# A group's tail in the attention layer is spread over more block steps

## The chip, the cores and the metric

The kernel runs on one core of a Trainium2 chip. The metric is the device time of one launch in microseconds (us), as the median of several launches. Before the change it is 2312.75 us, the median of 3 launches between 2312.53 and 2313.29.

## The reference

Four residual layers on a graph of 4096 nodes with 256 features, each preceded by a normalisation of the rows and a ReLU. Only the second layer, the attention, is touched:

```
h = maximum(layernorm(x), 0)
x = x + L0(h, adj)                       # A_norm @ (A2 @ h @ W.T)
h = maximum(layernorm(x), 0)
x = x + L1(h, adj)                       # the attention, below
h = maximum(layernorm(x), 0)
x = x + L2(h, adj)
h = maximum(layernorm(x), 0)
x = x + L3(h, adj)

L1:  h = x @ weight
     h_norm = h / maximum(norm(h), 1e-8)
     attn_logits = h_norm @ h_norm.T + log(adj + 1e-8)
     out = softmax(attn_logits, axis=1) @ h + bias
```

The numerators of the softmax are `(adj + 1e-8) * exp(cosine)`. `adj` is 4096 x 4096 in f32.

## The kernel before, in words

**Tiling.** Rows are taken in 8 groups of 512 (`NG`), the inner dimension in 32 blocks of 128 (`NB`), a group's rows in four row blocks of 128 (`GB`). f32 operands are split into two f16 halves, "hi" and "lo", and each product is three f16 matmuls: hi by hi, hi by lo, lo by hi. The program goes through six passes; pass 2 (`ATT`) is the attention, written out without loops. In the trace it lies between about 723 and 1320 us.

**One block step of the attention.** In step j of group g four engines work hand in hand:

- TensorE makes the cosines of block j + 3 (`LEAD`) in a PSUM bank (`similarity`, L1389 to L1391, six matmuls of 512 columns). The cosine matrix is symmetric, so blocks that an earlier group has made are fetched back and only transposed (L1375, four small matmuls). Then it multiplies block j (`product`, L1084 to L1086, twelve matmuls), which needs the lo half of the numerators of block j.
- ScalarE takes the exponential of block j where it is computed (L1846), then makes the hi half of block j - 1 (L1867).
- VectorE makes the numerators of block j (`numerators`, L2487, or L2494 in pieces) and then the lo half of block j - 1 (`lo_of_numerators`, L2502). Each engine executes its instructions in the order in which they are written.
- Beside that a sum S4 for a later pass is made out of the same blocks of `adj`: VectorE makes it in steps with j mod 4 = 3 (L2001) and its lo half in steps with j mod 4 = 1 (L2007), ScalarE its hi half in steps with j mod 4 = 0 (L1526). Groups 0 and 1 have one VectorE instruction more at each of the two (L1982, L1992).

**A group's tail.** When a group is through, its result goes through a chain of small pieces, which is interleaved with the block steps of the next group by the tables `ATT_PLACES`, one on each engine, indexed by the step j. Of the tail of group g - 1, in group g:

- VectorE: `epi0`, `epi1` (`attended`, L2149: x plus result over denominator, two row blocks each), `stats0`, `stats1` (L2401, two row blocks each), `stats2` (L2405 to L2408), `h0`, `h1` (L2414, lo half of the normalised rows), `mix0`, `mix1`, `mix2`, `W2` (L2310 to L2332, the combinations of the small product's result that the next pass multiplies by).
- ScalarE: `ev` (L1591), `h0` to `h3` (L1788, L1790), `W0` and `W1` (copies of the small products out of PSUM, L1715, and with `W1` the hi half of three quarters of them, L1738), `W2` (L1744).
- TensorE: `"W0W1"` at step `W_AT`, the small products by the next layer's weights (24 matmuls, L1295 to L1297), into the bank `psW` and into `psT`, which otherwise is one of three banks for the cosines. In the seven steps from `W_AT` on only the two banks `psS` are used for cosines.
- SyncE's queue, in half steps H (two block steps each): `send_x` stores x, `turn_h` turns the normalised rows with a DMA transpose (L778). Both wait for VectorE, and loads that come later in the queue wait behind them.

Group 7 (the last) has its own third table: the tail of group 6, but in place of the mixes two pieces that prepare the next pass (`sum`, `split0`).

Of the kernel before, what the change touches and what calls it, by code (L numbers as in the profile page):

```python
# [41 lines left out]
F = 256  # L42
P = 128
NB = N // P
GB = 4
# [37 lines left out]
def build(nc, x, adj_t, w0, wg, bias_g, w2, bias_2, w3a, w3b, sent, sums, ready, x_mid, directs, out):  # L83
    f32, f16 = mybir.dt.float32, mybir.dt.float16
    ALU, ACT = mybir.AluOpType, mybir.ActivationFunctionType

    ctx = ExitStack()
    with ctx:
        def sb(name, shape, dt):
            return ctx.enter_context(nc.sbuf_tensor(name, shape, dt))  # L90
# [4 lines left out]
        def sem(name):  # L95
            return ctx.enter_context(nc.semaphore(name))
# [15 lines left out]
        xs = left[:, spare:spare + GB * F].rearrange("p (b n) -> p b n", b=GB)  # L112
# [33 lines left out]
        ev = sb("ev", [P, GB, F + 1], f32)  # L146
# [50 lines left out]
        rden = sb("rden", [P, GB], f32)  # L197
# [60 lines left out]
        scaled = sem("scaled")  # L258
# [77 lines left out]
        def at(passes, p, g, per=1, k=1):  # L336
            return (g + NG * passes.index(p)) * per + k
# [118 lines left out]

            return sum(NB - GB * h for h in range(g)) + j - GB * g + 1

        W_AT = 23
        SIM_SLOT, SIM_BEFORE = [], []  # L460
        for n in range(NG * NB):
            last = {s: m for m, s in enumerate(SIM_SLOT)}
            s = min((0, 1) if n < NB or W_AT <= n % NB < W_AT + 7 else (0, 1, 2), key=lambda s: last.get(s, s - 3))
            SIM_SLOT.append(s)
# [100 lines left out]
        def _(sp):  # L565
# [76 lines left out]
            def store_s3(g, c):  # L642

                sp.wait_ge(s3_split, g * NC + c + 1)
                sp.dma_start(ready[bass.ds(g * (NC * P) + c * P, P), 4 * QUAD:6 * QUAD], out3[c % 4])\
                    .then_inc(s3_stored[c % 4], 16)

            def load_s2(n):

                if n >= S2_LATER * NC + 3:  # L650
                    sp.wait_ge(s4_split, n - 2)
                else:
                    sp.wait_ge(sum_ready, at(SELF, 1, NG - 1))
                sp.dma_start(s4_of(n), sums[n * P:(n + 1) * P, :]).then_inc(s2_back[n % 4], 16)
# [11 lines left out]
            def send_x(p, g):  # L666

                if p == 1:
                    sp.wait_ge(bias_added, g + 1)
                else:  # L670
                    sp.wait_ge(x_ready, at(RES, p, g))
                rows = x_rows(p, g).rearrange("p b n -> p (b n)")
                sp.dma_start(x_mid[bass.ds(g * P, P), :], rows).then_inc(x_stored, 16)
# [99 lines left out]
            def turn_h(p, g):  # L773

                sp.wait_ge(h_ready, at(SMALL, p, g))
                sp.wait_ge(small_ready, at(SMALL, p, g - 1, 2, 2))
                sp.sem_inc(turning, 1)
                sp.dma_start_transpose(hT[:, :, :], hsp[:, :, :, :].rearrange("p b s n -> p (b s n)"))\  # L778
                    .then_inc(hT_landed, 16)

            def turn_gn(g):

                sp.wait_ge(gn_ready, at([1], 1, g, GB, GB))
                sp.sem_inc(turning, 1)
                sp.dma_start_transpose(gnT[:, bass.ds(g * GB * 2 * FB, GB * 2 * FB), :],
                                       hsp[:, :, :, :].rearrange("p b s n -> p (b s n)")).then_inc(gnT_landed, 16)
# [124 lines left out]
            def att_extra(g, H):  # L911

                n = g * NH + H
                if n == 9 + NH:
                    for k in range(3):
                        load_s2(S2_LATER * NC + k)
                if g == 0:
                    if H < 4:
                        store_s3(NG - 1, H + 4)
                    if H == 4:  # L920
                        turn_gn(NG - 2)
                        send_x(1, NG - 2)
                    elif H == 8:
                        turn_h(1, NG - 1)
                    elif H == 10:
                        send_x(1, NG - 1)
                    elif H == 12:
                        turn_gn(NG - 1)
                else:
                    if H == 8:  # L930
                        send_x(ATT, g - 1)
                    elif H == 12:
                        turn_h(ATT, g - 1)

                if H == NH - 1:
                    fetch_x(ATT, g)

                if H % 2 == 0 and n >= 6:
                    store_s4((n - 6) // 2)
                    if (n - 6) // 2 < S2_LATER * NC:  # L940
                        store_s2((n - 6) // 2)
                    else:
                        load_s2((n - 6) // 2 + 3)
# [132 lines left out]
        def _(pe):  # L1076
# [173 lines left out]
            def small(p, g, r):  # L1250
# [10 lines left out]
                else:  # L1261

                    pe.wait_ge(hT_landed, 16 * at(TURN, p, g))
                    if p == ATT:
                        sim_taken(pe, max(n for n in range((g + 1) * NB + W_AT) if SIM_SLOT[n] == 2 or n == 0))

# [43 lines left out]

            ATT_PLACES = [{14: "W0W1"}, {W_AT: "W0W1"}]

# [34 lines left out]
            def similarity(g, j):  # L1347
# [7 lines left out]
                if SIM_SLOT[n] == 2:  # L1355
                    if n < NB + W_AT:
                        pe.wait_ge(gn_ready, at([1], 1, NG - 1, GB, GB))
                    else:
                        pe.wait_ge(small_copied, at(COPIED, ATT, (n - W_AT) // NB - 1, GB, GB))
                if computed(g, j):  # L1360
# [93 lines left out]
        def _(act):  # L1454
# [303 lines left out]
            def stage(name, p, g):  # L1758
# [12 lines left out]
                elif p in COPIED and name == "W2":  # L1771
# [2 lines left out]

            PLACES = {0: ["ev"], 4: ["h"], 5: ["k"], 6: ["W0", "W1"], 7: ["n0", "n1", "W2"]}
            ATT_PLACES = [{2: ["ev"], 10: ["h"], 15: ["W0"], 16: ["W1"], 18: ["n0"], 19: ["n1"]},
                          {2: ["ev"], 13: ["h0"], 14: ["h1"], 15: ["h2"], 16: ["h3"], 25: ["W0"], 26: ["W1"], 30: ["W2"]},
                          {2: ["ev"], 13: ["h0"], 14: ["h1"], 15: ["h2"], 16: ["h3"], 25: ["W0"], 26: ["W1"], 30: ["split0"]}]

            def att_h(g, b):  # L1780

# [144 lines left out]
        def _(dve):  # L1926
# [214 lines left out]
            def attended(g, i):  # L2141

                if i == 0:
                    dve.wait_ge(ev_ready, at(ALL, ATT, g, GB, GB))
                    nc.vector.reciprocal(rden[:, :], ev[:, :, F]).then_inc(den_ready, 1)
                    dve.wait_ge(x_back, 16 * at(BACK, ATT, g))
                    dve.wait_ge(den_ready, g + 1)
                for b in (2 * i, 2 * i + 1):
                    nc.vector.scalar_tensor_tensor(xs[:, b, :], ev[:, b, 0:F], rden[:, b:b + 1], xs[:, b, :],  # L2149
                                                   ALU.mult, ALU.add).then_inc(scaled, 1)  # L2150

            def last_mix():

# [54 lines left out]
            def epilogue(p, g):  # L2208

                if p in STR:  # L2210
                    dve.wait_ge(mixed, at(STR, p, g, NP, NP))
                    if p in ADDED:

                        dve.wait_ge(d_back, 16 * at(ADDED, p, g))
                        nc.vector.tensor_tensor(oq, oq, d_in, ALU.add).then_inc(turned_sum if p == TURNED else preact, 1)
                        return
                else:
                    dve.wait_ge(ev_ready, at(ALL, p, g, GB, GB))
                if p in SELF:

                    dve.wait_ge(own_ready, at(SELF, p, g))
                    nc.vector.tensor_tensor(o[:, :, :], ev[:, :, 0:F], own[:, :, :], ALU.add).then_inc(sum_ready, 1)
                    nc.vector.tensor_scalar(rowm[:, :], ev[:, :, F], 0.0, None, ALU.is_gt).then_inc(row_ready, 1)
                    nc.vector.tensor_scalar(rowc[:, :], ev[:, :, F], TINY, None, ALU.max).then_inc(row_ready, 1)
                    dve.wait_ge(sum_ready, at(SELF, p, g))
                if p == 1:
                    for b in range(GB):
                        nc.vector.tensor_scalar(o[:, b, :], o[:, b, :], d[:, blocks(g, b)], None, ALU.mult)\
                            .then_inc(scaled, 1)
                elif p == 2:  # L2230
                    for i in range(2):
                        attended(g, i)
                elif p == 3:
                    for b in range(GB):
                        nc.vector.scalar_tensor_tensor(o[:, b, :], o[:, b, :], dinv[:, blocks(g, b)], b2[:, :],
                                                       ALU.mult, ALU.add).then_inc(scaled, 1)
# [110 lines left out]
            def stage(name, p, g):  # L2347
# [28 lines left out]
                elif p == 1 and name in ("n0", "n1"):  # L2376
# [3 lines left out]
                      7: ["n0", "n1", "W2"]}  # L2380
            ATT_PLACES = [{2: ["ev"], 4: ["epi"], 6: ["x"], 7: ["stats"], 10: ["h"], 12: ["bias"], 15: ["W0"], 16: ["W1"],
                           18: ["n0"], 19: ["n1"]},
                          {4: ["epi0"], 6: ["epi1"], 8: ["stats0"], 9: ["stats1"], 10: ["stats2"],
                           16: ["h0"], 18: ["h1"], 26: ["mix0"], 28: ["mix1"], 30: ["mix2"], 31: ["W2"]},
                          {4: ["epi0"], 6: ["epi1"], 8: ["stats0"], 9: ["stats1"], 10: ["stats2"],
                           16: ["h0"], 18: ["h1"], 29: ["sum"], 31: ["split0"]}]
            LATE = {0: ["mix0", "mix1"], 1: ["mix2"], 2: ["W2"]}

            def att_piece(name, g):
# [245 lines left out]
```

## Time and profile before

| what | value |
|---|---|
| median of 3 launches | 2312.75 us |
| profiled launch | 2313.05 us, span 2311.3 us |
| TensorE (PE) matmul busy | 2289.8 us, 99% |
| VectorE (DVE) busy | 1693.5 us, 73% |
| ScalarE (ACT) busy | 1127.9 us, 49% |
| TensorE idle in the attention, by its waits | 4.0 us |

An instruction's row has its start, its duration, engine, line, what it writes and reads. In brackets stand the idle time of the engine before it and who ended that. Matmuls overlap: those of 258 columns last 0.27 us each but start every 0.11 us. Neighbours on VectorE and ScalarE overlap by about 0.1 us too, so that what one costs there is the distance between starts.

### The profile page before, as it was taken

What the parts mean: (1) busy time and instruction counts of PE and PEld (TensorE: products, weight loads), DVE (VectorE), ACT (ScalarE), POOL (GpSimd) and SP (SyncE); (2) the same over time, 40 slices, a digit from 0 to 9 for tenths busy, and PEclk for the clock granted to TensorE, in tenths of its full rate; (3) what the DMA queues carried; (4) which work ended last, traced back from release to release, by engine and by line L of the source; (5) the groups of instructions that cost most, each with busy time, mean ns of one, the idle gap of its engine ahead of it and who ended that gap; (6) DMA issues with size and microseconds to landing.
All of it is one profiled execution on the core that took longest, in us unless ns stands there. A gap on an engine that the chain in (4) does not pass through costs nothing.

```text
span 2311.3 us, 61483 instructions
## 1 busy us (share of the span) xinstructions
PE 2289.8 (99%) x24200; PEld 1896.5 (82%) x24200; DVE 1693.5 (73%) x2709; ACT 1127.9 (49%) x1806; POOL 145.9 (6%) x139
## 2 busy tenths in 40 slices
PE   7999999999999999999999999999999999999999
PEld 4555557888888677778888899999988888899999
DVE  7678677676677788778888876776766667667666
ACT  7444434445544555555555555455454444433332
POOL 3300110111111000000000000000000000000000
PEclk9999999999999999999999999999999999999999
DMA  9989998889887898989999998998998998999998
GB/s 336 334 276 330 350 337 305 284 261 281 264 268 229 261 287 288 288 270 312 333 310 330 338 351 310 332 330 310 331 349 307 330 343 301 340 344 383 374 377 301
DMA packets 294894, 727.17 MB, mean 315 GB/s; under 512 B 77024, under 2 KB 114656, under 8 KB 262112
## 3 DMA queue, kind: packets, MB, share of 16 engines
q1 hardware_dynamic: 294608, 724.95, 90.6%
q8 instruction: 97, 1.59, 0.3%
q14 instruction: 45, 0.37, 0.0%
q10 hardware_dynamic: 144, 0.26, 0.0%
HBM read 574.64 MB, written 138.41 MB: 309 GB/s over the span
## 4 chain that ended last, share of the span: by engine, by line
PE 90%; DVE 5%; issue 2%; ACT 1%; DMA 1%; POOL 0%; SPq 0%; DVEq 0%; POOLq 0%; ACTq 0%
PE acc L1084 9%; PE acc L1086 8%; PE acc L1085 8%; PE acc L1110 8%; PE acc L1106 8%; PE acc L1109 8%; PE acc L1096 4%; PE acc L1099 4%; PE acc L1098 4%; PE acc L1171 4%; PE acc L1172 4%; PE acc L1173 4%; PE psS L1389 2%; PE psS L1391 2%; PE psS L1390 2%
## 5 line engine op out<-in xcount | busy, mean ns | idle before, releaser
L1084 PE MATMUL acc<-right,ahi 128*128 128x258 f16 x1024 | 279.7, 273 | 3.2 <-DVE alo L2502 2.8
L1086 PE MATMUL acc<-right,alo 128*128 128x258 f16 x1024 | 279.6, 273 | 0.0
L1085 PE MATMUL acc<-right,ahi 128*128 128x256 f16 x1024 | 279.1, 273 | 0.0
L1106 PE MATMUL acc<-left,ahi 128*128 128x128 f16 x1536 | 270.5, 219 | 0.4 <-DVE alo L2020 0.4
L1109 PE MATMUL acc<-left,ahi 128*128 128x128 f16 x1536 | 270.4, 219 | 0.0
L1110 PE MATMUL acc<-left,alo 128*128 128x128 f16 x1536 | 270.4, 219 | 0.0
L1867 ACT ACTIVATE ahi<-en 128x512 f16<-128x512 f32 x256 | 160.2, 626 | 76.2 <-DVE en L2487 74.0
L2502 DVE SCALAR_TENSOR_TENSOR alo<-en,ahi 128x512 f16<-128x512 f32 x256 | 176.0, 687 | 4.1 <-ACT ahi L1867 4.1
L1106 PE MATMUL acc<-left,adj 128*128 128x128 f16 x1024 | 178.2, 219 | 0.0
L1106 PE MATMUL acc<-left,en 128*128 128x128 f16 x1024 | 178.2, 219 | 0.0
L1109 PE MATMUL acc<-left,adj 128*128 128x128 f16 x1024 | 178.2, 219 | 0.0
L1109 PE MATMUL acc<-left,en 128*128 128x128 f16 x1024 | 178.2, 219 | 0.0
L1110 PE MATMUL acc<-left,adj 128*128 128x128 f16 x1024 | 178.2, 219 | 0.0
L1110 PE MATMUL acc<-left,en 128*128 128x128 f16 x1024 | 178.2, 219 | 0.0
L1106 PEld LDWEIGHTS acc<-left,ahi 128*128 128x128 f16 x1536 | 150.3, 98 | 0.7 <-DVE alo L2020 0.6
L1109 PEld LDWEIGHTS acc<-left,ahi 128*128 128x128 f16 x1536 | 150.3, 98 | 0.0
L1110 PEld LDWEIGHTS acc<-left,alo 128*128 128x128 f16 x1536 | 150.3, 98 | 0.0
L1548 ACT ACTIVATE ahi<-en 128x512 f16<-128x512 f32 x191 | 118.6, 621 | 54.6 <-DVE en L2015 54.5
L1084 PE MATMUL acc<-left,ahi 128*128 128x258 f16 x512 | 139.8, 273 | 0.0
L1086 PE MATMUL acc<-left,alo 128*128 128x258 f16 x512 | 139.8, 273 | 0.0
L1084 PE MATMUL acc<-left,en 128*128 128x258 f16 x512 | 139.8, 273 | 0.0
L1086 PE MATMUL acc<-left,en 128*128 128x258 f16 x512 | 139.8, 273 | 0.0
(313 smaller groups left out, 7036.9 us busy)
## 6 DMA issues: line engine op xcount, KB each, us to landing
adj<-in_adj_t SPq DMA_DIRECT2D x194, 512.0 KB, 5.8
adj<-ready SPq DMA_DIRECT2D x96, 1024.0 KB, 7.8
en<-ready SPq DMA_DIRECT2D x96, 1024.0 KB, 8.2
en<-in_adj_t SPq DMA_DIRECT2D x32, 1024.0 KB, 8.9
adj<-in_adj_t SPq DMA_DIRECT2D x31, 1024.0 KB, 7.5
en<-ready SPq DMA_DIRECT2D x56, 512.0 KB, 5.4
en<-sent SPq DMA_DIRECT2D x46, 512.0 KB, 7.2
sent<-en SPq DMA_DIRECT2D x90, 256.0 KB, 4.1
```

What stands on the lines that cost most here:

```text
L1084: nc.tensor.matmul(acc[:, b, 0:n], hi, m[:, jb, 0:n], start=first, stop=False)
L1085: nc.tensor.matmul(acc[:, b, 0:F], hi, m[:, jb, LO:LO + F], start=False, stop=False)
L1086: return nc.tensor.matmul(acc[:, b, 0:n], lo, m[:, jb, 0:n], start=False, stop=last)
L1096: nc.tensor.matmul(to, bhi[:, cols], hi[:, rows], start=first and i % 2 == 0 and k == 0, stop=False, skip_group_check=True)
L1098: nc.tensor.matmul(to, bhi[:, cols], lo[:, rows], start=False, stop=False, skip_group_check=True)
L1099: last = nc.tensor.matmul(to, blo[:, cols], hi[:, rows], start=False, stop=False, skip_group_check=True)
L1106: nc.tensor.matmul(to, hi[:, rows], bhi[:, cols], start=first and i % 2 == 0 and b == 0 and k == 0, stop=False, skip_group_check=True)
L1109: nc.tensor.matmul(to, hi[:, rows], blo[:, cols], start=False, stop=False, skip_group_check=True)
L1110: last = nc.tensor.matmul(to, lo[:, rows], bhi[:, cols], start=False, stop=False, skip_group_check=True)
L1548: nc.scalar.activation(ahi[:, c % 2, 2 * QUAD:3 * QUAD], s1_of(p, g, c), ACT.Copy, scale=ADJ_SCALE)\
L1867: nc.scalar.activation(ahi[:, (j // GB) % 2, j % GB * GR:(j % GB + 1) * GR], nums[:, n % NUMS, :], ACT.Copy, scale=P_SCALE).then_inc(num_h ...
L2502: nc.vector.scalar_tensor_tensor(alo[:, (j // GB) % 2, cols], nums[:, n % NUMS, :], P_SCALE, ahi[:, (j // GB) % 2, cols], ALU.mult, ALU.su ...
```

## The change

The tail pieces stand at other steps, and the epilogue is cut finer. `attended` now does one row block per call and is called four times. On VectorE `epi0` to `epi3` stand at steps 4, 6, 8, 8 and the statistics at 10, 12, 14 (from 8, 9, 10); `h0`, `h1` at 18, 20 (from 16, 18); `mix0`, `mix1` at 28, 29 (from 26, 28); `mix2` and `W2` stay at 30 and 31. ScalarE's `h0` to `h3` move by three steps, its `W0`, `W1` by two, and so do the small products on TensorE (`W_AT` 23 to 25). `send_x` and `turn_h` move by one half step. No instruction is added or dropped in the tail but for the epilogue's grouping.

```diff
-        W_AT = 23
+        W_AT = 25
...
-                    if H == 8:
+                    if H == 9:
                         send_x(ATT, g - 1)
-                    elif H == 12:
+                    elif H == 13:
                         turn_h(ATT, g - 1)
...
-                for b in (2 * i, 2 * i + 1):
-                    nc.vector.scalar_tensor_tensor(xs[:, b, :], ev[:, b, 0:F], rden[:, b:b + 1], xs[:, b, :],
-                                                   ALU.mult, ALU.add).then_inc(scaled, 1)
+                nc.vector.scalar_tensor_tensor(xs[:, i, :], ev[:, i, 0:F], rden[:, i:i + 1], xs[:, i, :],
+                                               ALU.mult, ALU.add).then_inc(scaled, 1)
...
-                          {4: ["epi0"], 6: ["epi1"], 8: ["stats0"], 9: ["stats1"], 10: ["stats2"],
-                           16: ["h0"], 18: ["h1"], 26: ["mix0"], 28: ["mix1"], 30: ["mix2"], 31: ["W2"]},
+                          {4: ["epi0"], 6: ["epi1"], 8: ["epi2", "epi3"], 10: ["stats0"], 12: ["stats1"], 14: ["stats2"],
+                           18: ["h0"], 20: ["h1"], 28: ["mix0"], 29: ["mix1"], 30: ["mix2"], 31: ["W2"]},
```

VectorE in group 5, steps 8 to 10, before. L2487 makes numerators, L2502 their lo half, L2007 the lo half of S4, L2401 to L2408 the statistics:

```order
L2401 BN_STATS stats<-left 128x6 x2
L2487 SCALAR_TENSOR_TENSOR en<-adj,psS 128x512
L2502 SCALAR_TENSOR_TENSOR alo<-en,ahi 128x512
L2007 SCALAR_TENSOR_TENSOR left<-left 128x512
L2401 BN_STATS stats<-left 128x6 x2
L2487 SCALAR_TENSOR_TENSOR en<-adj,psT 128x512
L2502 SCALAR_TENSOR_TENSOR alo<-en,ahi 128x512
L2405 BN_AGGR mv<-stats 128x2 x4
L2407 TENSOR_SCALAR nmean<-mv 128x4
L2408 TENSOR_SCALAR vare<-mv 128x4
```

The same place after (each line of this part has moved up by one):

```order
L2400 BN_STATS stats<-left 128x6 x2
L2486 SCALAR_TENSOR_TENSOR en<-adj,psS 128x512
L2501 SCALAR_TENSOR_TENSOR alo<-en,ahi 128x512
L2001 TENSOR_TENSOR own<-adj,own 128x512
L2486 SCALAR_TENSOR_TENSOR en<-adj,psT 128x512
L2501 SCALAR_TENSOR_TENSOR alo<-en,ahi 128x512
L2400 BN_STATS stats<-left 128x6 x2
L2486 SCALAR_TENSOR_TENSOR en<-adj,psS 128x512
L2501 SCALAR_TENSOR_TENSOR alo<-en,ahi 128x512
```

Both pieces begin with `stats0`. `stats1` has left the step with the lo half of S4 (L2007); it stands two block steps behind `stats0` now, with the making of S4 (L2001) in the step between, and `stats2` follows two steps later.

VectorE at the end of group 5, before, from `mix1` (L2314, L2316) to `W2` (L2332); `mix0` stands further up:

```order
L2314 TENSOR_TENSOR left<-o,left 128x256
L2316 TENSOR_TENSOR left<-left,o 128x256
L2487 SCALAR_TENSOR_TENSOR en<-adj,left 128x512
L2502 SCALAR_TENSOR_TENSOR alo<-en,ahi 128x512
L2007 SCALAR_TENSOR_TENSOR left<-own,left 128x512
L2487 SCALAR_TENSOR_TENSOR en<-adj,en 128x512
L2502 SCALAR_TENSOR_TENSOR alo<-en,ahi 128x512
L2320 TENSOR_TENSOR left<-o,left 128x768
L2487 SCALAR_TENSOR_TENSOR en<-adj,en 128x512
L2502 SCALAR_TENSOR_TENSOR alo<-en,ahi 128x512
L2001 TENSOR_TENSOR left<-adj,left 128x512
L2332 TENSOR_TENSOR left<-left 128x1024
```

After, from `mix0` (L2309, L2310) to `mix2` (L2319); the numerators and lo half of one more block, L2001 and `W2` follow as before:

```order
L2309 TENSOR_TENSOR left<-o 128x256
L2310 TENSOR_TENSOR left<-o 128x256
L2486 SCALAR_TENSOR_TENSOR en<-adj,left 128x512
L2501 SCALAR_TENSOR_TENSOR alo<-en,ahi 128x512
L2007 SCALAR_TENSOR_TENSOR left<-own,left 128x512
L2313 TENSOR_TENSOR left<-o,left 128x256
L2315 TENSOR_TENSOR left<-left,o 128x256
L2486 SCALAR_TENSOR_TENSOR en<-adj,en 128x512
L2501 SCALAR_TENSOR_TENSOR alo<-en,ahi 128x512
L2319 TENSOR_TENSOR left<-o,left 128x768
L2486 SCALAR_TENSOR_TENSOR en<-adj,en 128x512
L2501 SCALAR_TENSOR_TENSOR alo<-en,ahi 128x512
```

`mix0` has come two block steps closer to the group's end, and `mix1` stands in the step with the lo half of S4.

ScalarE at the end of group 5, before: the two copies of the small products (L1715), the hi half of three quarters of them (L1738), and the exponential that follows (L1846):

```order
L1715 ACTIVATE o<-psW,dinv_w 128x2x128 x2
L1846 ACTIVATE en<-psS 128x512
L1867 ACTIVATE ahi<-en 128x512
L1715 ACTIVATE o<-psT,dinv_w 128x2x128 x2
L1738 ACTIVATE left<-o 128x768
L1846 ACTIVATE en<-psS 128x512
```

After:

```order
L1715 ACTIVATE o<-psW,dinv_w 128x2x128 x2
L1846 ACTIVATE left<-psS 128x512
L1867 ACTIVATE ahi<-en 128x512
L1526 ACTIVATE left<-own 128x512
L1715 ACTIVATE o<-psT,dinv_w 128x2x128 x2
L1738 ACTIVATE left<-o 128x768
L1846 ACTIVATE left<-psS 128x512
```

The hi half of S4 (L1526) now stands between the two copies, ahead of the exponential that follows them.

## Rows read from the trace of the kernel before

**Rows 1.** The page, busy time and instructions of TensorE, and its granted clock in 40 slices.

```profile
PE 2289.8 (99%) x24200; PEld 1896.5 (82%) x24200; DVE 1693.5 (73%) x2709; ACT 1127.9 (49%) x1806; POOL 145.9 (6%) x139
...
PEclk9999999999999999999999999999999999999999
```

**Rows 2.** Waits of TensorE from 723 to 1320 us: total, times, longest.

```profile
PE acc L1084 <- DVE alo L2502: 2.8, 6, 0.7
```

**Rows 3.** Timeline of TensorE, group 5, blocks 8 and 9 (start, us, engine, line).

```profile
1137.96 0.60 PE L1375 MATMUL psS<-ident,en 128*128 128x128 f32 x4
1138.40 0.27 PE L1084 MATMUL acc<-right,ahi 128*128 128x258 f16 x1
...
1139.71 0.60 PE L1375 MATMUL psS<-ident,en 128*128 128x128 f32 x4
1140.73 0.28 PE L1084 MATMUL acc<-right,ahi 128*128 128x258 f16 x1 [0.42 <-DVE alo L2502]
```

**Rows 4.** Timeline of VectorE, the same stretch.

```profile
1138.13 0.69 DVE L2007 SCALAR_TENSOR_TENSOR left<-left 128x512 f16<-128x512 f32 x1
1138.73 0.75 DVE L2401 BATCH_NORM_STATS2 stats<-left 128x6 f32<-128x256 f32 x2
...
1140.59 0.38 DVE L2405 BATCH_NORM_AGGREGATE mv<-stats 128x2 f32<-128x6 f32 x4
```

**Rows 5.** Timeline of TensorE where it waits: groups 1, 4, 7 and 7.

```profile
898.05 0.28 PE L1084 MATMUL acc<-right,ahi 128*128 128x258 f16 x1 [0.49 <-DVE alo L2502]
...
1068.88 0.28 PE L1084 MATMUL acc<-right,ahi 128*128 128x258 f16 x1 [0.42 <-DVE alo L2502]
...
1274.13 0.28 PE L1084 MATMUL acc<-right,ahi 128*128 128x258 f16 x1 [0.42 <-DVE alo L2502]
...
1317.06 0.28 PE L1084 MATMUL acc<-right,ahi 128*128 128x258 f16 x1 [0.65 <-DVE alo L2502]
```

**Rows 6.** Timeline of TensorE, end of group 5, and small products in group 7.

```profile
1171.41 0.27 PE L1295 MATMUL psW<-wsp,hT 128*128 128x256 f16 x1
...
1174.03 0.38 PE L1389 MATMUL psS<-right 128*128 128x512 f16 x1
...
1175.32 0.27 PE L1084 MATMUL acc<-right,ahi 128*128 128x258 f16 x1
...
1191.03 0.27 PE L1084 MATMUL acc<-right,ahi 128*128 128x258 f16 x1
...
1300.05 0.27 PE L1295 MATMUL psW<-wsp,hT 128*128 128x256 f16 x1
```

**Rows 7.** Timeline of ScalarE, end of group 5.

```profile
1173.65 0.60 ACT L1846 ACTIVATE en<-psS 128x512 f32<-128x512 f32 x1
...
1174.64 0.85 ACT L1715 ACTIVATE o<-psT,dinv_w 128x256 f32<-128x256 f32 x2
...
1176.32 0.58 ACT L1846 ACTIVATE en<-psS 128x512 f32<-128x512 f32 x1
...
1179.21 0.62 ACT L1526 ACTIVATE left<-own 128x512 f16<-128x512 f32 x1
```

**Rows 8.** Timeline of VectorE, end of group 5.

```profile
1177.00 0.69 DVE L2487 SCALAR_TENSOR_TENSOR en<-adj,en 128x512 f32<-128x512 f32 x1 [0.66 <-ACT en L1846]
...
1180.59 0.42 DVE L2316 TENSOR_TENSOR left<-left,o 128x256 f32<-128x256 f32 x1
...
1185.36 0.95 DVE L2320 TENSOR_TENSOR left<-o,left 128x768 f16<-128x768 f32 x1
...
1188.48 1.22 DVE L2332 TENSOR_TENSOR left<-left 128x1024 f16<-128x1024 f32 x1
...
1190.21 0.69 DVE L2502 SCALAR_TENSOR_TENSOR alo<-en,ahi 128x512 f16<-128x512 f32 x1
```

**Rows 9.** Timeline of VectorE, end of group 1.

```profile
894.25 0.68 DVE L1992 TENSOR_TENSOR left<-adj,left 128x512 f32<-128x512 f32 x1
...
895.58 1.22 DVE L2332 TENSOR_TENSOR left<-left 128x1024 f16<-128x1024 f32 x1
```

## What I expect of the change, and why

> **What bounds the kernel now.** I began with the page. TensorE is busy 99% of the span at the full granted clock [rows 1], so the end moves only by what TensorE waits more or less; what the other engines do is worth nothing unless TensorE stands for it. The waits of TensorE in the attention then give the size of the matter: the products there (L1084) wait for the lo halves of the numerators (L2502) for 2.8 us in all, six times [rows 2]. The timelines of TensorE say where. In the middle of group 5 the product of block 9 comes 1.02 us behind the transposes before it (1140.73 against 1139.71), where block 8 came 0.44 us behind its own (1138.40 against 1137.96): 0.58 us lost [rows 3], of which the bracket shows 0.42 as idle; the rest is the tail of the transposes, so a loss is the bracket plus 0.16. The same wait stands in groups 4 to 7, four times, first and last in [rows 5]: 2.3 us. One more of 0.65 us stands in front of group 1's last block, one of 0.8 us in front of group 7's [rows 5]. VectorE is behind in all of them. Its timeline shows the reason in the middle: the lo half of S4 and two pairs of statistics stand closely ahead [rows 4].
>
> **Prices.** A full-width VectorE instruction in a closed sequence costs 0.60 us (from 1138.13 to 1138.73), a pair of statistics 0.75 less the overlap of 0.1, so 0.65, and `stats2` (four aggregates of 0.38 together, two small ones) at most 0.6 [rows 4]. In the late part of a group whose blocks are transposed, a block costs TensorE 1.75 us (1139.71 less 1137.96 [rows 3]), and VectorE 1.2 for numerators and lo half, 1.8 where S4 comes in. So VectorE wins 0.55 us on a plain step and loses 0.05 on one with S4, and the tail pieces come out of that.
>
> **The middle of the group.** The epilogue is the same four instructions before and after and lies in steps 4 to 8 both times, so its price drops out. What leaves the steps up to 9 is `stats0` and `stats1`, 1.3 us. Where VectorE was 0.58 us late for block 9 it is now 0.7 us early. Steps 10 to 15 then take TensorE 6 x 1.75 = 10.5 us, VectorE 12 x 0.6 + 3 x 0.6 (S4) + 0.65 + 0.65 + 0.6 = 10.9 us, so 0.3 us of the lead is left. The pieces h0 and h1 at 18 and 20 stand in steps without S4 (0.55 of room for 0.6). The wait should go in all four groups: -2.3 us. Groups 1 to 3 have cosines with their 1.29 us instead of transposes there and no wait to lose. ScalarE's `h0` to `h3` stand at 16 to 19, two steps behind `stats2` in place of three; GpSimd's step between them fits, I take it as nothing, at most 0.4 us in each of groups 6 and 7 if VectorE has to wait for it. It is the thinnest cover: 0.3 us of lead.
>
> **SyncE's queue.** `send_x` and `turn_h` move by one half step, as their makers do by two block steps, and the small products by two, so the transposed rows have as many block steps as before. Loads and stores of their half step now stand ahead of them instead of behind. I count it as nothing; were the transpose late, the small products would wait for it, seven times.
>
> **The end of the group.** This is the term that decides. Call T the start of the small products. In group 5 before they start at 1171.41 and take 2.62 us, cosines 1.29 us, and the last block starts at 1191.03 without a wait, T + 19.62 [rows 6]; its lo half ends 1190.21 + 0.69 = 1190.90 [rows 8], only 0.13 us ahead. Now the small products start two blocks later, so that of these 19.62 us two blocks with their cosines, 2 x (1.31 + 1.29), lie ahead of T: the last block can start at T + 14.4.
>
> ScalarE cannot pass its copy `W0`, which waits for the small products, so all it does follows T. Exponential 28 comes at T + 2.24 (1173.65 [rows 7], there exponential 26); the hi half of block 27 follows; then the hi half of S4, which before came two steps later (0.62 less 0.1); then `W1` with its 1.68 us (1174.64 to 1176.32). Exponential 29 starts at T + 3.23 + 0.52 + 1.68 = T + 5.43, and numerators 29 follow 0.68 us behind (1176.32 to 1177.00 [rows 7, 8]): T + 6.11. From there VectorE has no more gap: numerators 29 to 31 and 0 of the next group and lo halves 28 to 30, seven of 0.6; S4 twice, 1.2; `mix1` two instructions of 0.42 with their wait, 0.8; `mix2` 0.95 less 0.1; `W2` 1.22 less 0.1, so 1.14; and the lo half of block 31, 0.69 [rows 8]. Together 8.9 us: it ends at T + 15.0, and TensorE starts about 0.06 behind. It is 0.65 us late, where it was not before. `mix0` is hidden: it fits into the time in which VectorE waits for exponential 29. Five groups (2 to 6): +3.3 us.
>
> Group 1 has one instruction more at each S4, 0.6 at the lo half and 0.7 at the making (894.25 to 895.58 are two of them, 1.33 [rows 9]): 1.3 us later still, 1.95 us of wait in place of 0.65: +1.3 us. Group 7 has no mixes, but `sum` (0.6) and `split0` (1.14), and its last blocks have no cosines beside them, so TensorE is fastest there. Its small products move from 1300.05 [rows 6] behind one set of transposes, one of cosines and two blocks: 0.44 + 1.29 + 2.62 later, 1304.4. With the same 5.43 us, exponential 29 is at 1309.8, its numerators at 1310.4 (a shorter exponential), and then VectorE has 7.6 us of work to the end of lo half 31: 1318.1 in place of the start at 1317.06 [rows 5]: +1.0 us.
>
> **Bounds of this term.** The trace has no group in which the S4 copy stands between the two copies, so both ends are worked out. If the copy finds a hole (it needs only what VectorE made one step earlier), it costs nothing and each end is 0.5 us better: 7 x 0.5 off, 2.1 us in place of 5.6. If `mix0`, which needs the copies of `W1`, is not hidden but comes on top (0.8 us in each group but the last, which has none), it is 5.6 + 4.8 = 10.4. I take 5.6: the nearest row, the closed sequence of [rows 7], speaks for copies one behind the other.
>
> **The sum.** -2.3 + 3.3 + 1.3 + 1.0 = +3.3 us. The profiled launch took 2313.05 us, so 2316.3 in its terms; the median of the launches is 0.3 lower, 2316.0. A measurement of this kernel can tell 0.2%, 4.6 us, from no change, so this is a small loss inside it.
>
> **Rivals.** *The ends absorb the moves*: the middle waits go and the ends stay as they were, because VectorE catches up in the time that the small products give. For it: before, VectorE idled 0.66 us before numerators 27 [rows 8]. Against it: that idle time lies ahead of the closed sequence, and the lead at the last block is 0.13 us already. It gives 2312.75 - 2.3 = 2310.4.
>
> *Slower*: the late copies hold up VectorE more than once. Its place is ScalarE's step 28 to 30, its price the 0.8 us of `mix0`, which waits for the copies out of `psT` and would lie on the path behind them in groups 1 to 6; it decides from the point where the copies end later than exponential 29 would be wanted, T + 5.4. The sum is then 10.4 - 2.3 = +8.1, 2320.9; half of it is past the 4.6 us. For it speaks that I found three ScalarE pieces in one step whose blocks are already the fast ones; against it the wait of 0.66 us that covers `mix0` in [rows 8].
>
> *Nothing happens*: what a group gains in the middle it waits at its end, because VectorE has the same work: 2312.75. Against it: after the middle TensorE does cosines again in groups 4 to 6 and VectorE has time over.
>
> *The clock*: waits at seven ends could cost TensorE its full granted clock. The row shows the full level, 2.4 GHz, in every slice, beside six waits of up to 0.8 us [rows 1, 5]. If after each end one block of 1.75 us ran at 1.2 GHz it would take twice that, 7 x 1.75 = 12.3 us more: 2328. The Trainium skill ("TensorE: Matmul & The Clock Gate", A second HAM failure mode: psum-queue depth-cycling) tells of a kernel that idled briefly between groups of matmuls and fell back and forth between the levels, with a loss of throughput. By that rule the change would pay this price; by the row, where such waits already stand and the level holds, it would not, and the row decides here.
>
> **How the numbers follow.** Forecast 0.47; ends absorb 0.13; nothing 0.04; slower 0.34; clock 0.02. Most of the forecast's own range, 2312.6 to 2317.4, is within 0.2%; with the first two and the third rival that makes 0.60 for no measurable change. Slower by over 0.2% 0.38: the slower rival, the clock and the edge of the forecast. Faster by over 0.2% 0.02: all six waits together are 3.8 us, less than 4.6. The range leaves out the half of the first rival's case below 2311.5 and what lies above the slower rival: 2311.5 to 2321.0.
>
> **What would show it.** In the changed profile the waits for L2501 at block 9 of groups 4 to 7 are gone; there are waits in front of the last block of groups 1 to 6, 0.5 us of idle in groups 2 to 6 and 1.8 in group 1; exponential 29 starts 5.4 us behind the start of the small products; group 7's last block waits 1.7 us. The prediction is wrong if VectorE is idle between numerators 29 and the last lo half, or if a wait comes up in blocks 12 to 20.

## The result and the profile after

The changed kernel takes 2316.24 us (median of 21 launches, 2315.57 to 2316.61), the kernel before, on the same chip, 2312.64 us (21 launches, 2312.19 to 2313.51). The ratio is 1.0015, with a 95% interval of 1.0009 to 1.0021: a loss of 3.6 us. The interval keeps clear of 1, so the loss is real, though it is inside the 0.2% that the prediction called no change. The profiled launch took 2316.16 us with a span of 2314.4 us, 3.1 us more than before. The page of the changed kernel, its row for TensorE and that of the granted clock, against [rows 1]:

```profile
PE 2291.2 (99%) x24200; PEld 1897.0 (82%) x24200; DVE 1692.8 (73%) x2709; ACT 1128.3 (49%) x1806; POOL 147.7 (6%) x139
...
PEclk9999999999999999999999999999999999999999
```

The work is the same and the clock stands at its full level, 2.4 GHz, in every slice. What has changed is how long TensorE waits for lo halves in the attention, 2.8 us in [rows 2] and now, in the view of waits:

```profile
PE acc L1084 <- DVE alo L2501: 5.4, 8, 1.7
```

Six waits have become eight, the longest 1.7 us in place of 0.7. They are not the same ones. TensorE's timeline in the middle of group 5 (start, duration, engine, line, operation), the place of [rows 3]:

```profile
1140.64 0.60 PE L1375 MATMUL psS<-ident,en 128*128 128x128 f32 x4
1141.08 0.27 PE L1084 MATMUL acc<-right,ahi 128*128 128x258 f16 x1
...
1142.39 0.60 PE L1375 MATMUL psT<-ident,en 128*128 128x128 f32 x4
1142.83 0.27 PE L1084 MATMUL acc<-right,ahi 128*128 128x258 f16 x1
```

Block 9 starts 0.44 us behind its transposes, as block 8 does; before it was 1.02. The 0.58 us are gone, in groups 4 to 7 alike. VectorE's timeline there, against [rows 4], has the statistics apart: one pair, the making of S4, the other pair, and the aggregates a step later again.

```profile
1142.03 0.74 DVE L2400 BATCH_NORM_STATS2 stats<-left 128x6 f32<-128x256 f32 x2
...
1143.88 0.68 DVE L2001 TENSOR_TENSOR own<-adj,own 128x512 f32<-128x512 f32 x1
...
1145.69 0.74 DVE L2400 BATCH_NORM_STATS2 stats<-left 128x6 f32<-128x256 f32 x2
...
1149.34 0.37 DVE L2404 BATCH_NORM_AGGREGATE mv<-stats 128x2 f32<-128x6 f32 x4
```

The waits that TensorE has now (in brackets the idle time ahead and who ended it), against [rows 5]. The first stands in front of the last block of group 1; the next three in front of that of groups 2, 5 and 6, and groups 3 and 4 have the same; the last two are in group 7:

```profile
899.32 0.28 PE L1084 MATMUL acc<-right,ahi 128*128 128x258 f16 x1 [1.73 <-DVE alo L2501]
...
978.08 0.28 PE L1084 MATMUL acc<-right,ahi 128*128 128x258 f16 x1 [0.52 <-DVE alo L2501]
...
1193.74 0.28 PE L1084 MATMUL acc<-right,ahi 128*128 128x258 f16 x1 [0.52 <-DVE alo L2501]
...
1258.77 0.28 PE L1084 MATMUL acc<-right,ahi 128*128 128x258 f16 x1 [0.51 <-DVE alo L2501]
...
1316.53 0.28 PE L1084 MATMUL acc<-right,ahi 128*128 128x258 f16 x1 [0.29 <-DVE alo L2501]
...
1320.20 0.28 PE L1084 MATMUL acc<-right,ahi 128*128 128x258 f16 x1 [0.85 <-DVE alo L2501]
```

With the 0.16 us that a bracket leaves out, group 1's end loses 1.89 us and each of groups 2 to 6 some 0.68 us. Adding up all places in the attention, to its last block, where two starts on TensorE lie further apart than the same two elsewhere gives 9.17 us, 5.85 before: 3.3 us more. Some 2.1 us of it lie in group 0 and are the same in every kernel here. This count is called "lost in the attention" below.

The end of group 5 shows the mechanism. The small products start at T = 1178.66 on TensorE. ScalarE's timeline behind them, the place of [rows 7]:

```profile
1180.18 0.84 ACT L1715 ACTIVATE o<-psW,dinv_w 128x256 f32<-128x256 f32 x2 [4.12 <-PE psW L1297]
1180.90 0.60 ACT L1846 ACTIVATE left<-psS 128x512 f32<-128x512 f32 x1
...
1181.90 0.64 ACT L1526 ACTIVATE left<-own 128x512 f16<-128x512 f32 x1
1182.42 0.85 ACT L1715 ACTIVATE o<-psT,dinv_w 128x256 f32<-128x256 f32 x2
1183.35 0.84 ACT L1738 ACTIVATE left<-o 128x768 f16<-128x768 f32 x1
1184.10 0.58 ACT L1846 ACTIVATE left<-psS 128x512 f32<-128x512 f32 x1
```

ScalarE stands for 4.12 us at the copy `W0`, and what is queued behind it, exponentials and hi halves among it, goes out in a burst. The hi half of S4 (L1526) lies between the copies, and exponential 29 starts at 1184.10. VectorE's timeline, the place of [rows 8]:

```profile
1183.31 0.42 DVE L2309 TENSOR_TENSOR left<-o 128x256 f32<-128x256 f32 x1 [0.38 <-ACT o L1715]
...
1184.79 0.69 DVE L2486 SCALAR_TENSOR_TENSOR en<-adj,left 128x512 f32<-128x512 f32 x1 [0.72 <-ACT left L1846]
...
1188.60 0.95 DVE L2319 TENSOR_TENSOR left<-o,left 128x768 f16<-128x768 f32 x1
...
1191.27 1.22 DVE L2331 TENSOR_TENSOR left<-left 128x1024 f16<-128x1024 f32 x1
...
1193.01 0.68 DVE L2501 SCALAR_TENSOR_TENSOR alo<-en,ahi 128x512 f16<-128x512 f32 x1
```

VectorE waits 0.38 us before `mix0` and 0.72 us before numerators 29; from there it has no gap until the last lo half ends at 1193.69, T + 15.03, and the block starts 0.05 us behind it.

### The profile page after: what moved, and what is told of

Its sections match the earlier page's. It is cut to its first block and busy times, and to the rows that moved or that the text cites. A ratio compares the mean times of both kernels' runs of the same rounds, so it can differ in the third digit from the quotient of the medians.

```text
span 2314.4 us, 61481 instructions
## 1 busy us (share of the span) xinstructions
PE 2291.2 (99%) x24200; PEld 1897.0 (82%) x24200; DVE 1692.8 (73%) x2709; ACT 1128.3 (49%) x1806; POOL 147.7 (6%) x139
```

## The experiments

Each is the changed kernel or the kernel before with the edit shown, timed beside the kernel before on the same chip; intervals are 95%. The ratio is to the kernel before on that chip: a median of 2312.64 us beside the changed kernel, 2312.87 beside the next four, 2312.93 beside the last three. The lines of the edits are shortened to the entries that differ.

| kernel | median us (lowest to highest, launches) | ratio to before (interval) | lost in the attention |
|---|---|---|---|
| before | 2312.64 (2312.19 to 2313.51, 21) | 1 | 5.85 |
| changed | 2316.24 (2315.57 to 2316.61, 21) | 1.0015 (1.0009 to 1.0021) | 9.17 |
| middle alone | 2310.41 (2309.88 to 2311.09, 11) | 0.9989 (0.998 to 0.9998) | 3.53 |
| ends alone | 2319.2 (2318.57 to 2319.4, 8) | 1.0027 (1.0016 to 1.0037) | 12.07 |
| mixes alone | 2312.94 (2312.07 to 2313.32, 11) | 1.0 (0.9991 to 1.0009) | 5.87 |
| S4's copy later | 2312.38 (2311.76 to 2313.73, 11) | 0.9998 (0.9989 to 1.0007) | 5.6 |
| small products at 24 | 2310.37 (2309.81 to 2310.67, 11) | 0.9989 (0.998 to 0.9998) | 3.54 |
| mixes early | 2309.75 (2308.95 to 2310.91, 11) | 0.9987 (0.9978 to 0.9996) | 3.09 |
| split last | 2309.66 (2309.05 to 2310.35, 11) | 0.9986 (0.9977 to 0.9995) | 2.07 |

**The middle alone.** The changed kernel with the pieces of the group's end put back to their old steps.

```diff
-        W_AT = 25
+        W_AT = 23
...
-                           27: ["W0"], 28: ["W1"],
+                           25: ["W0"], 26: ["W1"],
...
-                           28: ["mix0"], 29: ["mix1"],
+                           26: ["mix0"], 28: ["mix1"],
```

> The changed kernel with the small products, the copies W0 and W1 and the mixes back at their old steps (23, 25, 26, and 26 and 28); the epilogue by row blocks, the statistics at 10, 12, 14 and h0, h1 at 18, 20 stay. Theory (two independent terms, -2.3 us in the middle of groups 4 to 7 and +5.6 us at the ends): no wait in the middle, the ends as before the change, so 2.3 us faster than before, about 2310.3, ratio 0.9990. Rival (the work is the same, so what the middle gains is waited for at the end): same time as before, waits of 0.5 us in front of the last block of some groups. Rival (the transposed rows come late, since h1 is two steps later and the small products are not): TensorE waits in front of the small products, slower than before.

It took 2310.41 us, 2.5 less than the kernel before beside it, and 3.53 us are lost in the attention in place of 5.85. The waits for lo halves are down to two, in front of the last block of groups 1 and 7. The view of waits of this kernel:

```profile
PE acc L1084 <- DVE alo L2501: 1.1, 2, 0.6
```

The middle gives its 2.3 us when the end's pieces stay. The second rival, transposed rows that come late, costs nothing but is near: in group 7 the transpose lands at 1297.37 and the small products start at 1298.09, 0.7 us later, where the changed kernel has 4.1 us to spare (1302.48 and 1306.54).

**The ends alone.** The kernel before with only the end's pieces moved; the middle stays as it was.

```diff
-        W_AT = 23
+        W_AT = 25
...
-                           25: ["W0"], 26: ["W1"],
+                           27: ["W0"], 28: ["W1"],
...
-                           26: ["mix0"], 28: ["mix1"],
+                           28: ["mix0"], 29: ["mix1"],
```

> The kernel before with only the small products at 25, ScalarE's W0 and W1 at 27 and 28, mix0 and mix1 at 28 and 29. Theory: the four waits of 0.58 us in the middle stay and the ends wait as in the changed kernel (0.68 in groups 2 to 6, 1.3 more in group 1, 0.9 more in group 7): 5.6 us slower than before, about 2318.3, ratio 1.0024. Rival (the ends wait because the stretched middle leaves VectorE behind): the ends as before, no change.

It took 2319.2 us, 0.9 more than forecast. The ends lose what they lose in the changed kernel, to 0.01 us in each. Of the surplus the trace shows 0.6 us, in two places: the four waits in the middle are 0.64 to 0.65 us in place of 0.58, and group 7 has a new wait of 0.33 us ahead of its small products, the second of these rows of the ends-alone kernel (its view of waits, then TensorE's timeline):

```profile
PE acc L1084 <- DVE alo L2502: 7.5, 13, 1.7
```

```profile
1305.65 0.28 PE L1084 MATMUL acc<-right,ahi 128*128 128x258 f16 x1 [0.17 <-DVE alo L2502]
```

ScalarE there stands 3.79 us at the hi half of S4, waiting for a store of SyncE that is queued behind the DMA transpose of the small products' rows. The hi halves of numerators behind it come late, VectorE's lo half waits 2.13 us for one of them, and the product starts 0.06 us behind that lo half. ScalarE's, VectorE's and SyncE's rows (SPq is SyncE issuing a DMA):

```profile
1303.72 0.63 ACT L1526 ACTIVATE left<-own 128x512 f16<-128x512 f32 x1 [3.79 <-DMA ready<-left]
...
1304.90 0.69 DVE L2502 SCALAR_TENSOR_TENSOR alo<-en,ahi 128x512 f16<-128x512 f32 x1 [2.13 <-ACT ahi L1867]
...
1292.78 6.46 SPq L778 DMA_TRANSPOSE hT<-hsp  x1
...
1299.29 0.57 SPq L664 DMA_DIRECT2D ready<-left  x1
```

The kernel before has the same wait of ScalarE, 3.51 us, and TensorE loses nothing by it: the lo half that comes late there ends at 1300.49, while TensorE is at the small products, from 1300.05 on. The changed kernel, in which `turn_h` comes a half step later, has the store ahead of the transpose:

```profile
1289.15 0.44 SPq L664 DMA_DIRECT2D ready<-left  x1
...
1294.27 4.60 SPq L778 DMA_TRANSPOSE hT<-hsp  x1
```

**The turn later.** To test that reading: ends alone, and `turn_h` a half step later as in the changed kernel.

```diff
-                    elif H == 12:
+                    elif H == 13:
                         turn_h(ATT, g - 1)
```

> As e2_ends_alone, with turn_h at half step 13 in place of 12 and nothing else changed, for one look at the trace. Theory (in group 7 the DMA transpose, 6.5 us on SyncE's queue, holds back the store of S4's halves behind it; ScalarE's hi half of S4 waits 3.8 us for that store, and TensorE 0.33 us for what ScalarE does behind it): with the store ahead of the transpose ScalarE's wait for the store is gone, and so is the 0.33 us of TensorE in group 7; the other waits stay. Rival (the 0.33 us comes from the later small products themselves): ScalarE's wait goes, TensorE's stays.

There is one launch of it, so its time (2319.69 us beside 2312.26) tells nothing of so small a difference. Its trace lost 0.3 us less, 11.75 in place of 12.07: the 0.33 us of group 7 are gone, and so is ScalarE's wait for the store. ScalarE's timeline of this kernel, and below it SyncE's:

```profile
1301.15 0.63 ACT L1526 ACTIVATE left<-own 128x512 f16<-128x512 f32 x1 [0.57 <-DVE own L2001]
```

```profile
1292.50 0.42 SPq L664 DMA_DIRECT2D ready<-left  x1
...
1295.65 5.35 SPq L778 DMA_TRANSPOSE hT<-hsp  x1
```

The waits in the middle stayed at 0.64 to 0.65. Why they are 0.06 us longer than in the kernel before was not tried and stays open.

**The mixes alone.** The kernel before with `mix0` and `mix1` at 28 and 29 and nothing else: the prediction's rival for a clear loss lets `mix0` decide.

```diff
-                           26: ["mix0"], 28: ["mix1"],
+                           28: ["mix0"], 29: ["mix1"],
```

> The kernel before with only mix0 and mix1 at 28 and 29 in place of 26 and 28. Theory (the ends wait because everything that ScalarE does follows the later small products; the mixes fall into idle time of VectorE, 0.4 + 0.8 + 0.4 us in the last steps): no change, within 0.3 us. Rival (the ends wait because VectorE has the mixes packed against the group's end): 0.65 us or more in front of the last block of groups 1 to 6, 4 to 5 us slower than before.

No end got longer but group 1's, by 0.05 us, and 5.87 us are lost in the attention in place of 5.85. The time is that of before. The view of waits of this kernel has the row of [rows 2] with the same three numbers:

```profile
PE acc L1084 <- DVE alo L2502: 2.8, 6, 0.7
```

Where VectorE does its mixes costs nothing in this kernel, whose small products come at step 23. In the changed kernel `mix1`, 0.8 us, is part of the closed sequence behind exponential 29, and so of the chain.

**S4's copy later.** The changed kernel with the hi half of S4 at ScalarE's step 28 made one step later, behind `W1` and exponential 29, and its lo half on VectorE a step later too, in groups 1 to 7.

```diff
-                    if g * NB + j - 1 in S4_AT:
+                    if g * NB + j - 1 in S4_AT and not (g > 0 and j == 28):
                         hi_of_s4(S4_AT.index(g * NB + j - 1))
+                    if g > 0 and j == 29:
+                        hi_of_s4(S4_AT.index(g * NB + 27))
...
-                    if g * NB + j - 2 in S4_AT:
+                    if g * NB + j - 2 in S4_AT and not (g > 0 and j == 29):
                         lo_of_s4(S4_AT.index(g * NB + j - 2))
+                    if g > 0 and j == 30:
+                        lo_of_s4(S4_AT.index(g * NB + 27))
```

> The changed kernel, but in groups 1 to 7 the hi half of S4 of step 28 is made by ScalarE in step 29, behind exponential 29 and the hi half of block 28, and its lo half by VectorE in step 30 in place of 29. Theory: exponential 29 starts 4.9 us behind the small products' start in place of 5.4, the chain of VectorE behind it is as long as before, and the wait in front of the last block falls by 0.5 us in each of seven groups (0.68 to 0.15 in groups 2 to 6): 3.5 us faster than the changed kernel, about the time of the kernel before. Rival (the copy is not on the path; the number of VectorE instructions behind the small products sets the end): the waits stay at 0.68, same time as the changed kernel.

It took 3.9 us less than the changed kernel, and 3.5 us less are lost in the attention, as forecast. In group 5 the small products start at 1175.76. ScalarE's timeline of this kernel, then the start of the last block on TensorE:

```profile
1180.67 0.58 ACT L1846 ACTIVATE left<-psS 128x512 f32<-128x512 f32 x1
...
1181.67 0.62 ACT L1526 ACTIVATE left<-own 128x512 f16<-128x512 f32 x1
```

```profile
1190.32 0.28 PE L1084 MATMUL acc<-right,ahi 128*128 128x258 f16 x1
```

Exponential 29 is at T + 4.91, 0.53 us earlier than in the changed kernel (T + 5.44), and the last block at T + 14.56. The ends of groups 2 to 6 lose 0.15 us in place of 0.68, group 1's 1.47 in place of 1.89 with 0.09 a block earlier, group 7's 1.30 in place of 1.76. The chain from the copies through exponential 29 to the last lo half is thus what the ends wait for, and one copy of 0.52 us on it comes out, as 0.46 to 0.53 us, at each of seven ends.

**Small products at 24.** Halfway: all the pieces of the end one step ahead of where the change puts them.

```diff
-        W_AT = 25
+        W_AT = 24
...
-                           27: ["W0"], 28: ["W1"],
+                           26: ["W0"], 27: ["W1"],
...
-                           28: ["mix0"], 29: ["mix1"],
+                           27: ["mix0"], 28: ["mix1"],
```

> The changed kernel with the small products at 24, W0 and W1 at 26 and 27, mix0 and mix1 at 27 and 28: one step earlier than in the changed kernel, one later than before. Theory (a threshold: VectorE's closed sequence from the first numerators behind the copies must end before the last block could start): the last block can start at T + 17.0, and the S4 copy comes behind W1, so exponential 29 no longer waits for the copies; numerators 29 start at about T + 7.3, with 8.1 to 8.9 us of work the last lo half ends at T + 16.2 at most, in time. No wait at the ends of groups 2 to 6; 0.65 in group 1 and 0.8 in group 7 stay as before the change. Time as with the middle alone, 2310.4. Rival (the loss grows evenly with each step that the small products are moved): half of the end's loss, 2.8 us, is there, 2313.2.

It is as fast as with the end's pieces at their old steps: the first of the two steps is free, all the loss is in the second. The waits are the two of the middle-alone kernel, and in group 5 the last lo half ends 0.13 us ahead of the last block. The second step does two things: it takes 2.6 us from the time that VectorE has, and it puts the S4 copy ahead of `W1`, where at 24 it comes behind. As the run before shows, 3.5 us of the loss hang on that copy.

**Mixes early.** Middle alone, and the mixes and `W2` of groups 1 to 6 pulled ahead, to take them out of the sequence before the last lo half.

```diff
-                           25: ["W0"], 26: ["W1"], 30: ["W2"]},
+                           25: ["W0"], 26: ["W1"], 29: ["W2"]},
...
-                           26: ["mix0"], 28: ["mix1"], 30: ["mix2"], 31: ["W2"]},
+                           26: ["mix0"], 27: ["mix1"], 28: ["mix2"], 30: ["W2"]},
```

> The middle of the changed kernel, small products and copies at their old steps, and the mixes moved forward into VectorE's idle time: mix0, mix1, mix2 at 26, 27, 28 and W2 at 30 on VectorE, at 29 on ScalarE (before: 26, 28, 30, 31 and 30). Theory: VectorE's step 31 loses the 1.14 us of W2, the wait of 0.65 us in front of group 1's last block goes, nothing else changes: 0.65 us faster than the middle alone, 2309.8. Rival (W2 and mix2 meet the lo half of S4 and wait for ScalarE): no gain.

Group 1's wait of 0.66 us is gone and the median is 0.66 us lower than with the middle alone. A difference so small between two medians is not settled by 11 launches; the trace shows the wait gone, and also a new loss of 0.23 us in front of group 7's small products. They wait for the transposed rows: TensorE's weight load (PEld) stands until the transpose lands, 8.9 us after SyncE began to issue it. Both rows of this kernel:

```profile
1288.37 5.33 SPq L778 DMA_TRANSPOSE hT<-hsp  x1
...
1297.31 0.10 PEld L1295 LDWEIGHTS psW<-wsp,hT 128*128 128x128 f16 x1 [0.34 <-DMA hT<-hsp]
```

In the middle-alone kernel these rows had 0.7 us to spare; why the transpose takes longer here stays open. In all 3.09 us are lost in place of 3.53.

**Split last.** Mixes early, and in group 7 VectorE's piece of `split0` put behind the last lo half, to take away the last wait.

```diff
-                           18: ["h0"], 20: ["h1"], 29: ["sum"], 31: ["split0"]}]
+                           18: ["h0"], 20: ["h1"], 29: ["sum"]}]
...
                     lo_of_numerators(NG - 1, NB - 1)
+                    str_split_raw(STR[0], 0, 0)
                     lo_of_s1(STR[0], 0, 0)
```

> As e5_mixes_early, and in group 7 VectorE makes the last lo half before the 1.14 us of split0 instead of behind it. Theory: the wait of 0.81 us in front of group 7's last block goes, and split0 ends within the 1.3 us of that block, so the next pass starts as early: 2308.9 to 2309.0, 3.8 us faster than the kernel before, ratio 0.9984. Rival (the wait only moves on to the next pass's first products): as e5_mixes_early.

The forecast missed, and the rival was right on the time: nothing is gained that the medians show. It was wrong on the place. The wait of 0.81 us in front of group 7's last block is gone, and the next pass's first products, which need what `split0` makes, start without a wait (1314.19). A product 15 us further on waits longer. That product in the mixes-early kernel, and in this one:

```profile
1330.29 0.23 PE L1106 MATMUL acc<-left,ahi 128*128 128x128 f16 x1 [0.40 <-DVE alo L2020]
```

```profile
1329.65 0.23 PE L1106 MATMUL acc<-left,ahi 128*128 128x128 f16 x1 [1.04 <-DVE alo L2020]
```

What it waits for isn't `split0` but the fourth piece of the same kind. VectorE's rows of this kernel, `split0` and that fourth piece:

```profile
1312.41 1.22 DVE L2020 SCALAR_TENSOR_TENSOR alo<-wsp,ahi 128x1024 f16<-128x1024 f32 x1
...
1328.37 1.22 DVE L2020 SCALAR_TENSOR_TENSOR alo<-right,ahi 128x1024 f16<-128x1024 f32 x1
```

Between the two VectorE is idle for less than 1 us in either kernel, so the end of this stretch is set by the work in it and not by the order of two instructions at its start: the fourth piece starts 31.7 us behind the start of group 7's small products in both kernels. With the 0.16 us outside the bracket that is 0.56 and 1.20 us, and another product of that pass loses 0.17. So it was 0.81 + 0.56 us and is 1.20 + 0.17: 1.37 both times. The table's last column, which ends with the attention, doesn't see this; of its fall from 3.09 to 2.07, 0.81 us are the last block's wait and 0.2 the transpose, which lands in time here. These two kernels are the fastest of the study, some 3.2 us under the kernel before.

## Why the prediction was right

**The middle, -2.3 us.** Right, and shown by itself: the four waits are gone in the changed kernel, and with the middle alone 2.32 us less are lost in the attention, and the median falls by 2.5. The lead of VectorE was called thin, 0.3 us by block 15; in the trace of the changed kernel it is 0.38 us there in groups 5 to 7 and never under 0.2 in blocks 12 to 20 (from the lo half's end to its product's start), and no wait came up. The step of the sum that might have failed, GpSimd's and ScalarE's shorter distance behind `stats2`, cost nothing.

**SyncE's queue, nothing.** The sum holds: the small products of the changed kernel wait for no transpose. How near such a wait can be, the mixes-early kernel shows, which keeps the later rows and has the small products back at 23. But nothing was not quite what the move does. It puts the store ahead of the transpose and takes 3.5 us of waiting off ScalarE in group 7, and the pair of ends alone and turn later shows that with the late small products and without this move it comes through to TensorE with 0.33 us.

**The end of groups 2 to 6, +3.3 us.** Every point of the chain came out: exponential 29 at T + 5.44 for 5.43, numerators 29 at T + 6.13 for 6.11, the lo half's end at T + 15.03 for 15.0. The wait is 0.68 us for 0.65, five times 3.4. The S4 copy as part of the chain, which the prediction took over the bound in which it finds a hole, is shown by its removal.

**Group 1, +1.3 us.** 1.89 us at its last block and 0.09 a block earlier, against 0.65: +1.3.

**Group 7, +1.0 us.** The size is right, its shape is not. The prediction had one wait of 1.7 us in front of the last block. The profile has three, 0.29 us ahead of a block's transposes (1312.50), 0.46 at 1316.53 and 1.01 at 1320.20, together 1.76 against 0.82. The first, which the prediction had left out, is no wait for VectorE: these transposes need ScalarE's exponential 29, which starts at T + 5.43 there too and ends at 1312.45. ScalarE's row and TensorE's:

```profile
1311.97 0.47 ACT L1846 ACTIVATE en<-psS 128x384 f32<-128x384 f32 x1
...
1312.50 0.44 PE L1367 MATMUL psS<-ident,en 128*128 128x128 f32 x2
```

The other two are for lo halves. The last block's start is fixed by the last lo half, which ends at T + 13.6 (13.7 forecast), so what TensorE waits earlier it does not wait there, and the sum came out.

**The whole.** 3.3 us more lost in the attention, +3.1 in the span, +3.3 forecast; between the medians of this comparison it is +3.6. Ends alone against before is 6.2 us more in the attention, of which 5.6 are the ends and 0.6 the surplus told above.

**The rivals.** *Ends absorb* falls: its 2310.4 us is exactly what the kernel takes when the end's pieces stay, or move by one step only. *Nothing* falls with it. *Slower by `mix0`*: VectorE waits only 0.38 us for it, within the time in which exponential 29 isn't there yet, and the mixes alone cost nothing; the price of 0.8 us in six groups is not paid. It had got a third of the chance; the row that spoke against it, the idle time ahead of numerators 27, pointed the right way. *The clock*: waits of up to 1.9 us at seven ends left every slice at 2.4 GHz, with a mean of 0.999 of full speed. What the Trainium skill ("TensorE: Matmul & The Clock Gate", A second HAM failure mode: psum-queue depth-cycling) tells of a kernel whose idle moments between groups of matmuls threw the clock back and forth did not happen here: the trace shows no slice at the lower level.

## What to carry to other kernels

Where engines work in order, look at which instruction the moved work makes an engine stand at, and then count all that is queued behind it until the engine that bounds the kernel is served; that chain, counted from the start of the moved work, gave the end to 0.03 us. The cost of putting a piece later isn't proportional to the distance: it is nothing as long as the chain ends before the consumer comes (one step here). From there an instruction on the chain counts nearly in full in each group: the 0.52 us of the S4 copy came out as 0.46 to 0.53. What a further step would cost was not run. And a change that mends one place and loads another can be taken apart: half of this one gives 2.3 us, the other half takes 5.6.

## What was not expected of the hardware

Issuing the DMA transpose of the same rows in group 7 takes SyncE very different times: 4.60 us in the changed kernel, 5.35 with the turn later, 6.46 with the ends alone; in groups 1 to 6 of these kernels it is 1.8 to 4.2. A plain store queued behind it is issued only then (1299.29, 0.05 us after the transpose's issue ends), and a consumer of that store waits along: ScalarE for 3.5 to 3.8 us. What makes the issue long or short was not tried.

Where an engine works nearly without a gap, exchanging two of its instructions did not take a wait away but moved it: 0.81 us went from one block, and 0.81 us in all were added at two products of the next pass, most of it at one that waits for the end of the same stretch of work, 15 us later.
